# An LSTM on one core: the input product of two steps as seven half products in place of eight

## What is computed

```python
def step(carry, xw_t):
    prev_h, prev_c = carry
    a = xw_t + prev_h @ Wh
    i, f, o = sigmoid(a[:, :512]), sigmoid(a[:, 512:1024]), sigmoid(a[:, 1024:1536])
    g = tanh(a[:, 1536:])
    next_c = f * prev_c + i * g
    next_h = o * tanh(next_c)
    return (next_h, next_c), next_h
```

## Time and profile before

| | |
|---|---|
| median of three runs | 2726.98 us |
| the profiled execution itself | 2726.29 us |
| its span, first to last instruction | 2724.5 us |
| mean granted TensorE clock | 0.989 of full |
| PE busy | 2671.2 us (98%) |
| DVE busy | 1929.8 us (71%) |
| ACT busy | 1245.7 us (46%) |
| POOL busy | 45.9 us (2%) |

### The profile page before, as it was taken

How to read it: one execution, slowest core, us unless ns; L and a number is a source line. 1 busy time by engine, 2 the same in 40 slices (tenths; PEclk the granted TensorE clock), 3 DMA queues, 4 the chain that set the end, 5 groups by cost and what they waited for, 6 DMA issues and landing times.

```text
span 2724.5 us, 121148 instructions
## 1 busy us (share of the span) xinstructions
PE 2671.2 (98%) x49152; PEld 1387.0 (51%) x49152; DVE 1929.8 (71%) x8121; ACT 1245.7 (46%) x3722; POOL 45.9 (2%) x134
## 2 busy tenths in 40 slices
PE   3999999999999999999999999999999999999998
PEld 0455555555555555555555555555555555555554
DVE  6777777777777777777777777777777777777776
ACT  3444444444444444444444444444444444444444
POOL 0000000000000000000000000000000000000000
PEclk6999999999999999999999999999999999999999
DMA  6111111111111111111111111111111111111111
GB/s 144 37 43 35 38 38 40 35 39 42 35 38 38 40 35 39 42 35 38 38 39 35 39 42 35 39 38 39 35 39 42 35 39 39 38 35 39 42 36 26
DMA packets 223520, 109.94 MB, mean 40 GB/s; under 512 B 25216, under 2 KB 222464, under 8 KB 222464
## 3 DMA queue, kind: packets, MB, share of 16 engines
q1 hardware_dynamic: 223488, 109.48, 15.7%
HBM read 75.83 MB, written 33.55 MB: 40 GB/s over the span
## 4 chain that ended last, share of the span: by engine, by line
PE 97%; issue 1%; DVE 1%; DMA 1%; SPq 0%; ACT 0%; POOL 0%; DVEq 0%; POOLq 0%
PE Z L244 97%; DMA wx_raw<-in_Wx 1%; DVE wh_lo L435 0%; SPq L213 0%; SPq L200 0%; DVE wmax L417 0%; SPq L208 0%; DVE h_hi L475 0%; ACT tanh_c L356 0%; POOL wmax_all L537 0%; DVE xmax L396 0%; DVE x_lo L381 0%; DVE zs L407 0%; DVE c L490 0%; DVE scales L410 0%
## 5 line engine op out<-in xcount | busy, mean ns | idle before, releaser
L350 ACT ACTIVATE act<-Z,scales 128x192 f32<-128x192 f32 x1022 | 430.9, 422 | 1159.5 <-PE Z L244 1159.5
L244 PE MATMUL Z<-wx_hi,x_hi 128*32 128x512 f16 x8176 | 807.7, 379 | 9.3 <-DVE x_lo L381 9.3
L244 PE MATMUL Z<-wh_hi,hT_hi 128*32 128x512 f16 x8176 | 808.1, 379 | 8.0 <-DVE hT_hi L480 8.0
L244 PE MATMUL Z<-wh_lo,hT_hi 128*32 128x512 f16 x8176 | 808.1, 379 | 0.0
L244 PE MATMUL Z<-wx_hi,x_lo 128*32 128x512 f16 x8176 | 807.6, 379 | 0.0
L244 PE MATMUL Z<-wx_lo,x_hi 128*32 128x512 f16 x8176 | 807.6, 379 | 0.0
L244 PE MATMUL Z<-wh_hi,hT_lo 128*32 128x512 f16 x8176 | 533.1, 379 | 0.0
L486 DVE TENSOR_TENSOR fc<-act,c 128x64 f32<-128x64 f32 x512 | 115.3, 225 | 570.2 <-ACT act L350 570.2
L356 ACT ACTIVATE tanh_c<-c 128x64 f32<-128x64 f32 x1024 | 262.3, 256 | 269.7 <-DVE c L497 249.2
L475 DVE SCALAR_TENSOR_TENSOR h_hi<-act,scales,tanh_c 128x64 f16<-128x64 f32 x1024 | 291.3, 285 | 113.1 <-ACT tanh_c L356 86.3
L327 ACT ACTIVATE Z<-bias_bc,scales 128x512 f32<-128x512 f32 x511 | 344.6, 674 | 0.0
(11 more groups left out here) (50 smaller groups left out, 1286.1 us busy)
## 6 DMA issues: line engine op xcount, KB each, us to landing
x_in<-in_x SPq DMA_DIRECT2D x512, 64.0 KB, 2.0
x_res<-in_x SPq DMA_DIRECT2D x512, 64.0 KB, 2.1
out_y<-y SPq DMA_DIRECT2D x512, 64.0 KB, 1.7
wx_raw<-in_Wx SPq DMA_DIRECT2D x16, 256.0 KB, 8.8
wh_raw<-in_Wh SPq DMA_DIRECT2D x16, 256.0 KB, 19.0
bias_bc<-in_bias SPq DMA_DIRECT2D x4, 64.0 KB, 2.0
h_in<-in_h SPq DMA_DIRECT2D x4, 16.0 KB, 13.8
```

What stands on the lines that cost most here:

```text
L244: return nc.tensor.matmul(bank[L * j:L * j + B, :], lhsT, rhs, start=False, stop=last, skip_group_check=True)
L350: nc.scalar.activation(half_gates(act, a)[:, 0:3], half_gates(Z[s], a)[:, 0:3], ACT.Sigmoid, scale=scale).then_inc(sig_done, 1)
```

## The change

The steps are taken in pairs q (steps 2q and 2q + 1). For a pair, x is a 2 x 2 block matrix (step x half of the contraction) and Wx one too (half of the contraction x half of the gate columns); Strassen's method in Winograd's form gives the four result blocks with seven block products instead of eight. Each block product has two chunks of the contraction, three precision terms and four quarters, of 256 columns each: six groups of four matmuls of 256 columns.

- **Weights.** `wx_hi` and `wx_lo` hold seven forms (B11, B21, B22 and the sums T1 to T4). T1 to T4 are made on POOL from the raw weights in the prologue, 128 x 2048 float32 each. ScalarE cuts 14 high parts of 1024 columns, DVE 28 low parts of 512 columns. `TOP` becomes 12 for x and stays 14 for h.
- **x.** ScalarE scales x of a block (`scale_x`, 512 columns) into `forms`; DVE makes the sums S1 to S4 of it (four instructions of 128 columns per block); ScalarE cuts the high part for one pair at a time (`cut_x_hi`, 512 columns, now twice per block), DVE the low part (twice per block).
- **Result blocks.** There are eight banks: four `Z`, two `run`, two `extra`. ScalarE sets `run` and `extra` with bias, and copies `run` to the parts of `Z` in between products (`set_c11`, `set_c12`, `set_c21`, 256 columns each) and `extra` to SBUF (`take_p5`); DVE adds it with two instructions of 256 columns per pair (`add_extra`). `place_bias` is gone.
- **PE.** After the recurrent part of an even step come 21 groups of 256 columns (P7, P3, half of P5, and P1 of the pair after), after that of an odd step 21 groups (P6, P2, half of P5, and P4). PE's loop is over four steps.
- **Cell.** f c and i g of a half are one DVE instruction of 128 columns (`products`), which waits for sigmoid and tanh. The scales are read from copies (`h_scale`, `z_unscale`), set once per block.
- **Maximum of |x|** becomes the sum of |x|, on ScalarE (`sum_of_x`, Abs with accumulation).
- **y** = h + x moves from DVE to POOL, behind `h_lo_done`.
- The DMA lists are the same in number; x is loaded five blocks ahead.

```diff
-            def input_part(t, s, r):
...
+            def product(k, e, b, col, chunks=(0, 1)):
+                f, odd = x_form[k]
+                for cp in chunks:
                     for xp, wp in ((x_hi, wx_hi), (x_hi, wx_lo), (x_lo, wx_hi)):
                         for j in range(NJ):
+                            mm = add(b[L * j:L * j + B, col * HW:(col + 1) * HW], xp[:, e, 2 * f + cp, odd * B:(odd + 1) * B],
+                                     wp[:, k, cp, j * HW:(j + 1) * HW])
+                return mm
+
+            def first_product(q, e):
...
+                pe.wait_ge(x_lo_cut, q)
+                pe.wait_ge(run_set, q)
+                product(0, e, run[e], 0).then_inc(p1_done, 1)
+
+            def second_products(q, e):
+                pe.wait_ge(c11_set, q)
+                product(5, e, run[e], 0)
+                product(1, e, Z[2 * e], 0).then_inc(p2_done, 1)
+                pe.wait_ge(extra_set, q)
+                return product(4, e, extra[e], 0, (0,))
+
+            def third_products(q, e):
+                pe.wait_ge(c12_set, q)
+                product(6, e, run[e], 0).then_inc(p7_done, 1)
+                product(2, e, Z[2 * e], 1)
+                return product(4, e, extra[e], 0, (1,))
+
+            def last_product(q, e):
+                pe.wait_ge(c21_set, q)
+                pe.wait_ge(c22_set, q)
+                return product(3, e, Z[2 * e + 1], 0)
...
                     if started(t):
+                        if s % 2 == 0:
+                            pe.wait_ge(c12_added, q)
                         recurrent_part(t, s)
-                    if s < TB - 1:
-                        input_part(t + 1, s + 1, r)
...
+                    if s % 2 == 0:
+                            mm = third_products(q + 1, 1 - e)
+                            mm.then_inc(p5_done, 1)
+                            first_product(q + 2, e)
+                    else:
+                            second_products(q + 2, e)
+                            mm = last_product(q + 1, 1 - e)
+                            mm.then_inc(slot_done, 1)
```

ScalarE's list behind its five (before) or six (after) instructions of the step, and DVE's:

```diff
+                    if s == 0:
+                            take_p5(2 * n + 1, 1)
+                            set_c21(2 * n + 1, 1)
+                            scale_x(n + 2, r)
+                            set_c11(2 * n + 2, 0)
+                    if s == 1:
+                            cut_x_hi(2 * n + 3, n + 1, 1 - r, 1)
+                            set_c12(2 * n + 2, 0)
+                            set_run(2 * n + 3, 1, 1 - r)
+                            set_extra(2 * n + 3, 1, 1 - r)
+                    if s == 2:
+                            take_p5(2 * n + 2, 0)
+                            set_c21(2 * n + 2, 0)
+                            set_c11(2 * n + 3, 1)
+                            sum_of_x(n + 3, 1 - r, i + 2 + r)
+                    if s == 3:
+                            cut_x_hi(2 * n + 4, n + 2, r, 0)
+                            set_c12(2 * n + 3, 1)
+                            set_run(2 * n + 4, 0, r)
+                            set_extra(2 * n + 4, 0, r)
+                            set_z_unscale(n + 1, 1 - r)
```

```diff
-                    add_x(n, i, s, r)
...
+                    step(n * TB + s)
+                    if s == 0:
+                            add_extra(2 * n + 1, 1)
+                            first_forms(n + 2, r)
+                    if s == 1:
+                            cut_x_lo(2 * n + 3, 1 - r, 1)
+                            turn_x(n + 3, 1 - r, i + 2 + r)
+                    if s == 2:
+                            add_extra(2 * n + 2, 0)
+                            last_forms(n + 2, r)
+                            set_h_scale(n + 1, 1 - r)
+                    if s == 3:
+                            cut_x_lo(2 * n + 4, r, 0)
+                            scale_block(n + 3, 1 - r)
```

POOL's prologue, and DVE's in the order of its list:

```diff
             share_xmax(0)
+            nc.gpsimd.tensor_tensor(t3[:, :, :], w_block(1, 1), w_block(0, 1), ALU.subtract).then_inc(t3_made, 1)
+            pool.wait_ge(raw_done, 1)
+            pool.wait_ge(wmax4_done, NCH)
+            nc.gpsimd.tensor_tensor(w_block(0, 1), w_block(0, 1), w_block(0, 0), ALU.subtract).then_inc(t1_made, 1)
+            pool.wait_ge(wmax_done, 1)
+            nc.gpsimd.partition_all_reduce(wmax_all[:, 0:1], wmax[:, 0:1], P, ...).then_inc(wmax_shared, 1)
+            nc.gpsimd.tensor_tensor(t2[:, :, :], w_block(1, 1), w_block(0, 1), ALU.subtract).then_inc(t2_made, 1)
+            pool.wait_ge(wx_lo_cut, 2 * 2)
+            nc.gpsimd.tensor_tensor(w_block(1, 0), w_block(1, 0), t2[:, :, :], ALU.subtract).then_inc(t4_made, 1)
...
+                set_h_scale(0, 0)
+                first_forms(0, 0)
+                last_forms(0, 0)
+                cut_wh_lo(0)
+                cut_x_lo(1, 0, 1)
+                cut_wh_lo(1)
+                first_forms(1, 1)
+                last_forms(1, 1)
+                cut_wh_lo(2)
+                cut_wh_lo(3)
+                turn_x(2, 0, 2)
+                cut_x_lo(2, 1, 0)
+                scale_block(2, 0)
```

More of the change, by code:

```diff
@@ L93, in lstm_residual @@
         scales = sb("scales", [P, 2, 4], I32)
+        h_scale = sb("h_scale", [P, 1])
+        z_unscale = sb("z_unscale", [P, 1])
         Z = [bank(f"Z{s}") for s in range(TB)]
+        run = [bank(f"run{e}") for e in range(2)]
+        extra = [bank(f"extra{e}") for e in range(2)]
         wx_loaded = [sem(f"wx_loaded{ch}") for ch in range(NCH)]
@@ L258, in _ @@
                 raw = by_tile(wx_raw[:, ch])
[L259 to L260 removed]
+                for s in range(2):
+                    for j in range(NJ):
+                        mm = add(Z[s][L * j:L * j + B, :], x0_T[:, ch, s, :], raw[:, j])
+            mm.then_inc(raw_done, 1)
             pe.wait_ge(h0_turned, 1)
@@ L313, in _, with sum_of_x @@
+            block(0)
+            with pe.Fori(1, NB - 2) as n:
+                block(n)
+            block(NB - 2)
+            block(NB - 1)
         @block_ctx.scalar
         def _(sc):
-            def cut_x_hi(n, r, busy):
+            def sum_of_x(n, r, count):
+                sc.wait_ge(x_loaded[r], 16 * NJ * count)
+                if started(n):
+                    sc.wait_ge(xmax_shared, n)
+                nc.scalar.activation(x_abs[:, :], x_in[:, r].rearrange("p t c -> p (t c)"), ACT.Abs,
+                                     accum_out=xmax[:, :]).then_inc(xmax_done, 1)
@@ new lines, in cut_x_hi, with set_run @@
+            def cut_x_hi(q, n, r, e):
+                sc.wait_ge(s4_done, n + 1)
+                if started(q - 2):
+                    sc.wait_ge(slot_done, q - 2)
+                nc.scalar.activation(x_hi[:, e], forms_of_pair(r, e), ACT.Copy).then_inc(x_hi_cut, 1)
+            def set_run(q, e, r):
+                if started(q - 2):
+                    sc.wait_ge(c22_set, q - 2)
+                nc.scalar.activation(run[e][:, 0:HW], bias_bc[:, 0:HW], ACT.Copy, scale=z_scale(r)).then_inc(run_set, 1)
@@ new lines, in set_extra, with set_c11, set_c12 @@
+            def set_extra(q, e, r):
+                if started(q - 2):
+                    sc.wait_ge(p5_taken, q - 2)
+                nc.scalar.activation(extra[e][:, 0:HW], bias_d[:, :], ACT.Copy, scale=z_scale(r)).then_inc(extra_set, 1)
+            def set_c11(q, e):
+                sc.wait_ge(p1_done, q)
+                nc.scalar.copy(Z[2 * e][:, 0:HW], run[e][:, 0:HW]).then_inc(c11_set, 1)
+            def set_c12(q, e):
+                sc.wait_ge(p2_done, q)
+                nc.scalar.copy(Z[2 * e][:, HW:], run[e][:, 0:HW]).then_inc(c12_set, 1)
@@ new lines, in set_c21, with take_p5, set_z_unscale @@
+            def set_c21(q, e):
+                sc.wait_ge(p7_done, q)
+                nc.scalar.copy(Z[2 * e + 1][:, 0:HW], run[e][:, 0:HW]).then_inc(c21_set, 1)
+            def take_p5(q, e):
+                sc.wait_ge(p5_done, q)
+                if started(q - 1):
+                    sc.wait_ge(c22_set, q - 1)
+                nc.scalar.copy(p5[:, :], extra[e][:, 0:HW]).then_inc(p5_taken, 1)
+            def set_z_unscale(n, r):
+                sc.wait_ge(scales_done, n + 1)
+                nc.scalar.copy(z_unscale[:, :], scales[:, r, 3:4].bitcast(F32)).then_inc(z_unscale_set, 1)
@@ L336, in _, with cut_wx_hi @@
-            sc.wait_ge(w_scale_done, 2)
-            for ch in range(NCH):
+            def cut_wx_hi(k, made):
+                if made is not None:
+                    sc.wait_ge(made, 1)
+                for cp in range(2):
+                    nc.scalar.activation(wx_hi[:, k, cp].rearrange("p (j g c) -> p j g c", g=2, j=NJ),
+                                         w_form[k][:, cp].rearrange("p (g j c) -> p j g c", g=2, j=NJ), ACT.Copy,
+                                         scale=w_scale[:, 0:1].bitcast(F32)).then_inc(wx_hi_cut, 1)
```

428 lines of the change are left out of this document (265 added, 163 removed).

## The result

The changed kernel took 3549.04 us (median of 4, 3542.66 to 3554.55) against 2727.36 (4 runs, 2726.51 to 2727.76): ratio 1.301, 95% interval 1.299 to 1.304. Forecast were 2669 us, between 2640 and 2725. The profiled execution took 3542.66 us.

The account below looks back on a forecast made before the run. The prediction took PE, streaming without a gap, as the bound, with the chain through h right behind it and bounding the changed step. Summed: 2726.3 - 76.5 (steps) + 18.7 (prologue) + 0.2 (tail) = 2668.7, said as 2669 us, range 2640 to 2725.

Parts of the forecast that it names:

- y on POOL: In the loop, y on POOL is awaited only by the next step's h, 4 us on: no cost unless longer.
- A: Rival, PE's 21 small groups: each costs more than half a large one, 0.14 us, giving 2924 us; chance 11%.
- B: Rival, ACT in the loop: Abs isn't in the sigmoid and tanh table, so tables reload, 2863 us; chance 4%.
- PE's work: PE per step: 256-column input groups at 0.1092 us, sum 4.883 us, 0.297 less than before.
- The chain: Path through h per step: 2.66 us to the recurrent matmul, period 5.03 us, saving 76.5 us over 510 periods.
- E: Rival, each step: the chain through h is shorter than read and PE stays the bound, 2594 us; chance 3%.
- hT_lo late next, no second stall: PE's recurrent part: 0.17 of 0.19 us of cover at hT_lo is used, so no second stall opens.
- Side work on ACT and DVE: Loop copies, additions and forms: hidden, with 0.5 us to spare on ACT and 0.4 on DVE at worst.
- Prologue: Before step 1: later weights' maximum +6.7, more low cuts +8.0, DVE's path +4.0, together +18.7 us.
- third term: Prologue, DVE's path to step 1: forms, x_lo, x_T, scale block and h_scale, less one maximum, +4.0 us.
- D: Rival, prologue: DVE stands still while POOL makes T2 and T4, adding 7.2 us, 2676 us; chance 27%.
- C: Rival, loop: side work doesn't fit, DVE needs 2.3 of 2.06 us at s = 2, +31, 2700 us; chance 12%.

Follow-up runs that it names:

- e2_before_y_pool: The kernel before the change, with y moved to POOL and the maximum over partitions behind the second y of a block: 3558.91 us.
- e1_y_dve: The changed kernel with y = h + x moved back from POOL to DVE: 2701.33 us.
- e3_share_copy: The changed kernel with the loop's maximum over partitions replaced by a POOL copy of the same 128 x 1 tile: 2699.36 us.
- e9_less_pe: The changed kernel with y on DVE and the second chunk of P4 left out, three of 21 small groups after every odd step: 2701.08 us.

## Why the prediction was wrong, step by step

- **The step that failed** is "y on POOL: nothing, unless it takes longer than that". It set the addition alone (it takes 0.45 us) against 4 us of cover. The term that was missing is POOL's change of kind, 6.3 + 7.2 us in each block, placed between y and y of two steps that DVE's h waits for. Measured alone it is 833 us on the kernel before (e2_before_y_pool), 848 in the changed one (e1_y_dve). None of my rivals had it; A and B, the two that would have been far slower, were wrong in mechanism. In the loop of the kernel before POOL only makes maxima; its one change of kind, from the memsets at the start to the first maximum, lies inside a wait of 29.83 us, so no row showed a price. The Trainium skill comes near it (GPSIMD Engine Reference, Instruction dispatch): the first call to a freshly loaded kernel pays a code load of some 6 us, measured as 5.95 from a MODIFY_POOL_CONFIG record on, with no instruction in the profile to show it. The trace agrees in size and in the record: such records at every change (e3_share_copy), and gaps of 5.8 to 6.9 us one way; the way back, 6.6 to 7.9, is longer than that figure. That two kinds which alternate pay again each time is what the runs add. I used that page for the price of an addition and not for this. That loading of code is what fills the gap is the page's account; the runs show that the gap depends on the two kinds following each other.
- **PE's work**: right. Groups of 256 columns are 0.109 us apart (20 distances from 1201.89 to 1204.07), so A falls.
- **The chain**: R to the first recurrent matmul was forecast at 2.66 us and is 1204.35 - 1201.68 = 2.67; the period 5.03 and is 5.06. Two errors cancelled: the matmul starts 0.05 us behind the transpose, not 0.15, and the merged product costs 0.14 instead of 0.03. The first error comes of reading a loop from step 1: in the changed kernel too step 1 has 0.14 (104.29 to 104.43), at a granted clock of 1.00, so it is not the half clock that the earlier trace rows were taken at; why step 1 differs is not shown. "Half of the freed time is gained" was right for the wrong parts, and the part that could be mended was on the list of edits: without the merge the step is 4.92 us, where PE's sum is 4.883. e9_less_pe shows the chain as the bound, so E falls.
- **hT_lo late next, no second stall**: right. The first group on hT_lo starts 1206.09 - 1204.35 = 1.74 us behind the first of the eight before it, 8 x 0.2158 = 1.73.
- **Side work on ACT and DVE**: hidden, as forecast; the 256-column additions take 0.40 and 0.42 us for my 0.45.
- **Prologue**: forecast +18.7 us; the first recurrent matmul of step 1 starts at 104.43 instead of 70.38, +34.1. (The forecast's third term adds up to 3.8, not 4.0.) T3 and T1 took 4.5 us each, my 4.6. What was missing was again the change of kind, and D was half right. POOL, then DVE, in the changed kernel's prologue:

```profile
33.72 4.49 POOL L826 TENSOR_TENSOR wx_raw<-wx_raw 128x2048 f32<-128x2048 f32 x1
44.30 0.38 POOL L828 PARTITION_ALL_REDUCE wmax_all<-wmax  x1 [6.08 <-issue]
51.78 12.37 POOL L830 TENSOR_TENSOR t<-wx_raw 128x2048 f32<-128x2048 f32 x1 [7.11 <-issue]
64.23 4.50 POOL L834 TENSOR_TENSOR wx_raw<-wx_raw,t 128x2048 f32<-128x2048 f32 x1
83.02 0.38 POOL L836 PARTITION_ALL_REDUCE wmax_all<-wmax  x1 [14.29 <-DVE wmax L656]
```

```profile
54.41 2.73 DVE L672 SCALAR_TENSOR_TENSOR wx_lo<-t,w_scale,wx_hi 128x512 f16<-128x512 f32 x4
...
65.37 5.90 DVE L672 SCALAR_TENSOR_TENSOR wx_lo<-t,w_scale,wx_hi 128x512 f16<-128x512 f32 x4 [5.57 <-ACT wx_hi L519]
...
82.72 0.16 DVE L656 TENSOR_REDUCE wmax<-wmax 128x1 f32<-128x4 f32 x1
```

The maximum starts 6.1 us behind T1, at 44.30 instead of 37.0 (the last chunk of Wx was also 1.2 us later than before). T2 starts 7.1 us behind the maximum. It takes 12.4 us where T1 takes 4.5, while DVE's low cuts of two SBUF operands run at their usual 2.73 for four: POOL was the one held up. Beside T4 it is DVE, four cuts take 5.90. The Trainium skill (SBUF — State Buffer, Who interferes with whom) says that a DVE instruction with two SBUF inputs contends with a GpSimd one that reads SBUF, and that the shared ports are an exclusive lock. The trace agrees in both cases, and in both the engine already at work kept its pace: T2 is 7.9 us longer beside 8.0 us of DVE cuts that were running when it started (51.78 to 59.80), and the four cuts are 3.2 us longer behind a T4 that had started before them and runs 3.4 us on (65.37 to 68.73). D had it the other way round for T2. The late maximum (7.3 us), DVE's wait for the forms (5.57) and the slowed cuts (3.2) are 16 us together, for 15.4 more than forecast.

The last POOL row shows when a change costs nothing: its two MODIFY_POOL_CONFIG records come at 68.92, right behind T4, and the maximum starts 0.14 us behind the DVE result it waits for (82.72 + 0.16). The gap runs from the end of the instruction before, and here it lies inside a wait of 14.29 us.

- **B** (Abs) and **C** (side work) did not happen: two table loads in all, both ahead of the loop (the second at 99.72), no ACT or DVE instruction of the side lists ahead of a late chain except the scales, and these because the maximum was late. By its own terms C's s = 2 would have needed 2.23 us, not 2.3: +22 instead of +31.

Without y on POOL my sum would have read 2669 for a measured 2701: 15 us of that in the prologue, the other half 0.03 us in each of 510 steps.

## What to carry to other kernels

An engine that a trace shows with one kind of work has no price in it for a second kind. Before an addition is moved to an idle POOL that also makes maxima over partitions, ask what follows what in its list, and who waits across the change: here 0.45 us of work in each step cost 6.6 us per block, and a second buffer for h took most of it back. A change costs nothing where POOL would have waited as long anyway. And where a chain through small instructions stands 0.2 us behind the bound, merging two of them into one can cost more than it saves, once the bound moves to the chain.

## What the runs showed of the hardware

- POOL stood 5.7 to 7.1 us from an addition or subtraction (TENSOR_TENSOR) to the maximum over partitions, and 6.6 to 8.1 us the other way, wherever no longer wait covered it (all traces; 5.8 to 6.9 and 6.6 to 7.9 in the changed kernel); between addition and copy nothing (1209.30 behind 1208.85 + 0.46). The profile calls it "issue", or names a DMA that had nothing to do with it. Two MODIFY_POOL_CONFIG records stand at each change.
- A POOL instruction of two SBUF operands and a row of DVE instructions of two SBUF operands did not run together: T2 beside 8.0 us of cuts took 12.37 instead of 4.5 us, four cuts beside T4 5.90 instead of 2.73.
- While PE stood for 4.4 us at hT_lo its granted clock fell to 0.50 (1.2 GHz), and its groups of 256 columns came 0.21 us apart instead of 0.11; the step after the stall took 6.22 instead of 5.06 us at a mean granted clock of 0.80.
- Three of 42 small groups per pair of steps (e9_less_pe) can go without any effect on the time of a kernel whose PE is busy 97% of the span (e1_y_dve; 100.00 of the 100 us from 1200 to 1300). That PE waits for hT_hi all the same, 233.8 us in 1009 times by its weight loads; the wait does not show as idle time, since the recorded matmuls (0.28 to 0.4 us) are longer than the distance from one group to the next.
